# A pre-norm attention and mixture-of-experts layer on one core: the router's product, its logits and the order of some queues are changed

## The chip, the core and the metric

The kernel runs on one core of a Trainium2 chip. TensorE (PE) multiplies, VectorE (DVE), ScalarE (ACT) and GpSimd (POOL) work elementwise, SyncE (SP) issues most of the DMAs. Each engine takes its instructions strictly in the order written and waits on semaphores. The metric is the device time of one execution in microseconds (us).

## The reference, cut to what matters

`x` is 8 x 2048 tokens of 256 numbers, float32.

```python
x = x + attn(layernorm(x))            # linear attention: K^T V per sequence, then Q times it
y = layernorm(x)                      # x2 in the kernel
scores = sigmoid(y @ Wr)              # 256 -> 8 router scores
idx = top_k(scores + router_bias, 2); w = scores[idx] / (sum + 1e-9); cw = scatter(w)
hid = silu(y @ Wg[e]) * (y @ Wu[e])   # e = 0..3, inner width 128
routed = sum_e cw[e] * (hid @ Wd[e]) + (cw[4] + cw[6]) * y + cw[7] * relu(y)
out = x + routed + causal_conv4(y) + conv_b
```

## The kernel before, in words

The 16,384 tokens are 32 groups of 512 (four tiles of 128 tokens; eight sequences of four groups). One body is written out for each of the steps n = 7 to 39; the head does the steps before. In one step different stages work on different groups, as `LAG` says: L (statistics and norm 1), A (Gram matrix and transposes of the normed input), Q (query projection), B (attention product, residual, norm 2), R (transposes of x2, router, routing weights), C (the four experts), Y (the last expert's down product, output). So a group that passes B in step n passes R in n+1 and C in n+2. Every fourth step (n = 9, 13, ... 33) is a chain step, in which the matrix of a new sequence is also made out of the Gram matrix (`chain_gramT`, `chain_p1`, `chain_et`, `chain_f`). In the last steps stages go off one after the other: L after n = 31, A after 32, B after 36, R after 37, C after 38.

Products that must be exact are made in float32r out of a high part, which ACT copies, and a remainder (`_lo`), which DVE or POOL subtracts: `three` issues three passes. `gate_up(st, k)` is 2 x 3 passes of 512 columns for one expert's gate (k even) or up (k odd) product; `down(st, stage, e)` is 12 passes of 256 columns and waits for `hid_lo` of expert e. The chain of one expert is: PE gate and up products, ACT `silu`, POOL `gate_weight` (times the routing weight `cwb`), DVE `hidden`, ACT `hid_high`, then `hid_low` (DVE for experts 0 and 2, POOL for 1 and 3), PE `down`.

The routing of the next group runs beside it, in each step: PE `x2_transpose` 0 and 1 with `down(Y, 3)` between them, `gate_up` 2, `router` (eight float32 matmuls of 8 columns, the transposed x2 as weights; L509), ACT `logits_copy`, POOL `power` (e to the minus logits with ALU.pow, L1287, and plus one, L1291), DVE `route` (L1025 to L1052, top 2 and weights `cw`), PE `weights_transpose`, ACT `weights_copy`, SP a DMA to HBM (L333) and one DMA (L340) that spreads the four rows over all partitions into `cwb`, for which POOL's `gate_weight(0)` of the next step waits.

The hand-written orders that matter: on POOL `gate_weight` 0 and 1, `power`, `gate_weight` 2, `hid_low` 1, `norm1_factors`, `gate_weight` 3, the DMA that adds relu to `acc` (L1318), `norm2_factors`, `hid_low` 3, `skip_factors`. On DVE `conv_tap` 0, `norm1_stats`, `x2T_low` 0, `conv_tap` 1, `x2T_low` 1, `output`, `hidden` 0, `conv_tap` 2, `hid_low` 0, `hidden` 1, `hidden` 2, `route`, `hid_low` 2, `residual`, `norm2_stats`, `hidden` 3, `q_low`, `xnT_low`. `residual` needs the attention product alone, but stands behind `route` in DVE's queue.

Of the kernel before, what the change touches and what calls it, by code (L numbers as in the profile page):

```python
# [92 lines left out]


# [9 lines left out]
def program(nc, x, wq, wkT, wvT, woT, wr, rbias, wg, wu, wd, convwb, cw_rows, out):  # L104
# [17 lines left out]
    with ctx:  # L122
# [15 lines left out]
        wr_sb = sb("wr_sb", [P, HC, NE])  # L138
        wgu_hi = sb("wgu_hi", [P, 2, EM, HC, I], F32R)
# [41 lines left out]
        logits = sb("logits", [P, TG * NE])  # L181
# [44 lines left out]
        cwb_loaded = [sem(f"cwb_loaded{k}") for k in range(2)]  # L226
# [40 lines left out]
        halo_ready = sem("halo_ready")  # L267
        router_done = sem("router_done")
        logits_ready = sem("logits_ready")
# [42 lines left out]
        def _(sp):  # L312
# [15 lines left out]
            def spread_weights(st):  # L328
# [59 lines left out]
        def _(pe):  # L388
# [74 lines left out]
            def xn_transpose(st, c):  # L463
# [10 lines left out]
                elif g == 2:  # L474
                    if c == 0:
                        pe.wait_ge(logits_ready, 1)
# [61 lines left out]
            def attention(st, h):  # L538
# [10 lines left out]
                else:  # L549
                    pe.wait_ge(logits_ready, st.before("R", 1, 1))  # L550
# [52 lines left out]
            def head():  # L603
# [25 lines left out]
                router(r)  # L629
                xn_transpose(at("A", 2, NG), 0)  # L630
# [18 lines left out]
            def body(st):  # L649
                c_on, y_on, r_on, a_on, b_on, m_on = (st.on("C"), st.on("Y"), st.on("R"), st.on("A"), st.on("B"),  # L650
                                                      st.chain())
                if c_on and st.later("C", 1):
# [29 lines left out]
                if b_on and not m_on:  # L682
# [5 lines left out]
                if b_on:  # L688
# [22 lines left out]
        def _(act):  # L711
# [36 lines left out]
            def split_weights():  # L748
                act.wait_ge(w_loaded, 16 * N_LOADS)
                copy(wgu_hi[:, 0].rearrange("p e c i -> p (e c i)"), wg_st.rearrange("p e c i -> p (e c i)"))\  # L750
# [89 lines left out]
            def head():  # L840
# [22 lines left out]
                logits_copy(r)  # L863
                xnT_high(at("A", 2, NG), 0)
# [14 lines left out]
            def body(st):  # L879
# [19 lines left out]
                if m_on:  # L899
                    f_copy(st)  # L900
                if c_on:
                    hid_high(st, 0)
                if c_on:
                    silu(st, 2)

# [9 lines left out]
                    hid_high(st, 1)  # L915
# [7 lines left out]
                if r_on:  # L923
                    weights_copy(st)
                if st.on("Q"):
# [7 lines left out]
                if st.on("B"):  # L933
# [7 lines left out]
        def _(dve):  # L941
# [17 lines left out]
            def hid_low(st, e):  # L959

                dve.wait_ge(hidhi_ready, st.before("C", EM, e + 1))
                v.tensor_tensor(hid_lo[:, 0], hid[:, 0], hid_hi[:, 0].bitcast(F32), ALU.subtract)\
                    .then_inc(hidlo_ready[0], 1)
# [111 lines left out]
            def split_weights():  # L1075

                dve.wait_ge(w_loaded, 16 * N_LOADS)
                dve.wait_ge(whi_ready, NSPLIT)
# [286 lines left out]
```

## Time and profile before

| | |
|---|---|
| median of three runs | 924.8 us (924.77 to 928.49) |
| the profiled execution | 928.5 us, span of its instructions 926.7 us |
| granted TensorE clock, mean | 0.982 |
| PE busy | 881.6 us, 95% |
| DVE busy | 690.0 us, 74% |
| POOL busy | 608.5 us, 66% |
| ACT busy | 602.5 us, 65% |

The busy times are unions over the span. The matmuls overlap, so a busy PE says that something was in the array, not how dense it was. The clock is a share of 2.4 GHz.

### The profile page before, as it was taken

Reading aid. Unit: us, or ns where it says so; the run is one execution under the profiler, and the core shown is the slowest. Engines: PE = TensorE matmul, PEld = TensorE weight load, DVE = VectorE, ACT = ScalarE, POOL = GpSimd, SP = SyncE. Lnnn points to the kernel's source line nnn. Section 1 sums busy time; section 2 is a strip of 40 time slices with the busy share of each in tenths; the row PEclk is TensorE's granted clock in tenths of the full one; section 3 lists DMA queues with packets and bytes.
Section 4 is the critical chain, followed back from the end, with each engine's and each line's share of the span. In section 5 each row is a group of like instructions: output and inputs, shape, how many; then the busy total and the mean of one; then the engine's idle time right before and its main releaser. Section 6 shows DMA issues by size and latency. Waiting matters only on the chain.

```text
span 926.7 us, 16363 instructions
## 1 busy us (share of the span) xinstructions
PE 881.6 (95%) x5402; PEld 767.2 (83%) x5402; DVE 690.0 (74%) x1998; ACT 602.5 (65%) x1212; POOL 608.5 (66%) x686
## 2 busy tenths in 40 slices
PE   5779999999999999999999999999999999988896
PEld 4668888888888888888898888888888888777785
DVE  5766878977787888778779877877887776666563
ACT  5675676677677667766766776676677656644543
POOL 3236776667677666777766676786667767665663
PEclk9888999999999999999999999999999999999999
DMA  9111434434234443334344442434443322333232
GB/s 288 42 69 29 130 116 137 138 115 122 62 123 128 138 137 114 102 90 129 115 138 138 119 132 52 132 115 138 137 117 113 92 69 93 112 115 107 77 92 67
DMA packets 65620, 103.83 MB, mean 112 GB/s; under 512 B 4992, under 2 KB 57344, under 8 KB 61440
## 3 DMA queue, kind: packets, MB, share of 16 engines
q1 hardware_dynamic: 60928, 86.01, 27.4%
q0 software_dynamic: 4608, 16.78, 9.6%
q8 instruction: 43, 0.70, 0.3%
q14 instruction: 41, 0.34, 0.1%
HBM read 68.96 MB, written 17.04 MB: 93 GB/s over the span
## 4 chain that ended last, share of the span: by engine, by line
PE 53%; POOL 31%; DVE 5%; ACT 5%; issue 4%; DMA 1%; POOLq 0%; ACTq 0%; DVEq 0%
POOL enx L1287 17%; POOL gate L1254 8%; PE ps_gu L391 6%; PE ps_gu L393 6%; PE ps_gu L392 6%; PE ps_gram L457 6%; PE ps_y L391 5%; PE ps_y L392 4%; PE ps_y L393 4%; POOL hid_lo L1259 4%; PE ps_sh L482 3%; PE ps_gram L459 3%; PE ps_sh L499 3%; ACT gate L720 2%; PE ps_gu L532 2%
## 5 line engine op out<-in xcount | busy, mean ns | idle before, releaser
L1254 POOL TENSOR_TENSOR gate<-gate,cwb 128x512 f32<-128x512 f32 x128 | 165.3, 1292 | 113.8 <-ACT gate L720 74.8
L391 PE MATMUL ps_gu<-x2T_hi,wgu_hi 128*128 128x512 f32 x512 | 212.2, 414 | 3.3 <-DVE hid L956 3.3
L393 PE MATMUL ps_gu<-x2T_hi,wgu_lo 128*128 128x512 f32 x512 | 203.2, 397 | 0.0
L392 PE MATMUL ps_gu<-x2T_lo,wgu_hi 128*128 128x512 f32 x512 | 202.4, 395 | 0.0
L1287 POOL TENSOR_TENSOR enx<-inv_e,logits 128x32 f32<-128x32 f32 x32 | 177.1, 5535 | 10.6 <-ACT logits L713 10.4
L956 DVE TENSOR_TENSOR hid<-ps_gu,gate 128x512 f32<-128x512 f32 x128 | 86.2, 673 | 123.8 <-POOL gate L1254 101.7
L391 PE MATMUL ps_y<-wd_hi,hid_hi 128*128 128x256 f32 x512 | 157.2, 307 | 6.6 <-POOL hid_lo L1259 3.1
L393 PE MATMUL ps_y<-wd_hi,hid_lo 128*128 128x256 f32 x512 | 145.8, 285 | 0.0
L392 PE MATMUL ps_y<-wd_lo,hid_hi 128*128 128x256 f32 x512 | 145.8, 285 | 0.0
L973 DVE SCALAR_TENSOR_TENSOR conv<-x2T,conv_w,conv 128x512 f32<-128x512 f32 x192 | 144.2, 789 | 0.0
L391 PEld LDWEIGHTS ps_gu<-x2T_hi,wgu_hi 128*128 128x128 f32 x512 | 97.3, 190 | 22.7 <-DVE hid L956 6.8
L393 PEld LDWEIGHTS ps_gu<-x2T_hi,wgu_lo 128*128 128x128 f32 x512 | 97.1, 190 | 22.4
L720 ACT ACTIVATE gate<-ps_gu 128x512 f32<-128x512 f32 x128 | 76.1, 595 | 60.7 <-PE ps_gu L393 60.7
L391 PEld LDWEIGHTS ps_y<-wd_hi,hid_hi 128*128 128x128 f32 x512 | 98.5, 192 | 20.7 <-POOL hid_lo L1259 20.1
L392 PEld LDWEIGHTS ps_gu<-x2T_lo,wgu_hi 128*128 128x128 f32 x512 | 97.4, 190 | 13.6
L1259 POOL TENSOR_TENSOR hid_lo<-hid,hid_hi 128x512 fp32r<-128x512 f32 x64 | 83.4, 1303 | 35.0 <-ACT hid_hi L713 34.8
L713 ACT ACTIVATE hid_hi<-hid 128x512 fp32r<-128x512 f32 x128 | 79.9, 624 | 34.6 <-DVE hid L956 34.6
L1232 POOL TENSOR_TENSOR mv<-mv,eps_ln 128x4 f32<-128x4 f32 x64 | 12.5, 195 | 132.9 <-DVE mv L1005 113.4
L392 PEld LDWEIGHTS ps_y<-wd_lo,hid_hi 128*128 128x128 f32 x512 | 98.5, 192 | 0.1
L393 PEld LDWEIGHTS ps_y<-wd_hi,hid_lo 128*128 128x128 f32 x512 | 98.1, 192 | 0.0
L781 ACT ACTIVATE xn<-xa,shift,rstd 128x256 f32<-128x256 f32 x128 | 66.3, 590 | 23.6 <-POOL shift L1237 23.5
L457 PE MATMUL ps_gram<-xn 128*128 128x256 f32 x256 | 77.7, 386 | 0.0
(103 smaller groups left out, 1837.6 us busy)
## 6 DMA issues: line engine op xcount, KB each, us to landing
cwb<-cw_rows SPq DMA_DIRECT2D x32, 1024.0 KB, 4.7
xa<-in_x SPq DMA_DIRECT2D x32, 512.0 KB, 6.9
acc<-in_x SPq DMA_DIRECT2D x32, 512.0 KB, 6.0
acc<-x POOLq DMA_DIRECT2D x32, 512.0 KB, 4.6
out<-acc SPq DMA_DIRECT2D x64, 256.0 KB, 2.3
cwb<-in_wg SPq DMA_DIRECT2D x4, 128.0 KB, 3.8
cwb<-in_wu SPq DMA_DIRECT2D x4, 128.0 KB, 3.6
cwb<-in_wd SPq DMA_DIRECT2D x1, 512.0 KB, 4.5
```

The lines of the kernel that those rows point to most:

```text
L391: nc.tensor.matmul(dst, a_hi, b_hi, start=start, stop=False, skip_group_check=True)
L392: nc.tensor.matmul(dst, a_hi, b_lo, start=False, stop=False, skip_group_check=True)
L393: return nc.tensor.matmul(dst, a_lo, b_hi, start=False, stop=stop, skip_group_check=True)
L457: nc.tensor.matmul(ps_gram[:, 0:H], xn[:, q, t, 0:P], xn[:, q, t, :], start=start, stop=stop, skip_group_check=True)
L713: return nc.scalar.activation(dst, src, ACT.Copy, scale=scale)
L720: nc.scalar.activation(gate[:, e % 2], ps_gu[GU_BANK[2 * e]][:, :], ACT.Silu)\
L781: nc.scalar.activation(xn[:, q, t], xa[:, q, t], ACT.Identity, bias=shift1[:, f, t:t + 1], scale=rstd1[:, f, t:t + 1]).then_inc(xn_ready, 1)
L956: v.tensor_tensor(hid[:, e % 2], ps_gu[GU_BANK[2 * e + 1]][:, :], gate[:, e % 2], ALU.mult)\
L973: v.scalar_tensor_tensor(conv[:, c], x2T[:, q, c, k:k + GT], conv_w[:, c, k:k + 1], conv[:, c], ALU.mult, ALU.add).then_inc(conv_ready, 1)
L1254: g.tensor_tensor(gate[:, e % 2], gate[:, e % 2], cwb[:, q, e], ALU.mult).then_inc(gatew_ready, 1)
L1259: g.tensor_tensor(hid_lo[:, 1], hid[:, 1], hid_hi[:, 1].bitcast(F32), ALU.subtract)\
L1287: g.tensor_tensor(enx[:, :], inv_e[:, :], logits[:, :], ALU.pow).then_inc(enx_ready, 1)
```

## The change: what it does

The router's product is turned round: the router's weights, split into a high part and a remainder side by side (`wr2`, 16 of 128 columns used, the rest zero), become the stationary operand, and four float32r passes of 512 columns give the transposed logits. The first pass needs the high part of x2T's first half, the last needs the second half's remainder. ACT copies 16 x 512 of it, PE transposes it in four pieces of 16 rows behind `gate_up(3)`, ACT copies the pieces (`parts_copy`), and POOL adds the two halves of 8 at the head of `power`. `hid_low(1)` goes from POOL to DVE, and ACT's `hid_high(1)` goes ahead of the skip and relu work. The spreading DMA becomes four, one for an expert, each with its own semaphore. In the steps in which C is on and A is not, other than a chain step (`drain`, n = 34 to 38), PE makes the attention products around `gate_up(4)`, DVE does residual and statistics ahead of `hidden(2)`, POOL issues the relu DMA and the norm 2 factors ahead of `gate_weight(3)`, ACT does norm 2 right behind `weights_copy`; where B is off (n = 37), `route` stands ahead of `hidden(2)`.

```diff
+    def drain(self):
+        return self.on("C") and not self.on("A") and not self.chain()
...
-                sp.dma_start(cwb[:, k].rearrange("p e n -> p (e n)"),
-                             rows.rearrange("a e n -> (a e n)").partition_broadcast(P))\
-                    .then_inc(cwb_loaded[k], 16)
+                for e in range(EM):
+                    sp.dma_start(cwb[:, k, e], rows[0, e].partition_broadcast(P)).then_inc(cwb_loaded[k][e], 16)
...
             def router(st):
-                pe.wait_ge(x2T_ready, st.before("R", HC, HC))
+                if st.before("R") == 0:
+                    pe.wait_ge(wrlo_out, 1)
+                b, q = ps_sh[0], st.slot("R", 2)
                 pe.wait_ge(x2Tlo_ready, st.before("R", HC, 1))
-                b, q = ps_sh[0], st.slot("R", 2)
+                for c in range(HC):
+                    if c == 1:
+                        pe.wait_ge(x2Thi_ready, st.before("R", HC, HC))
+                    nc.tensor.matmul(b[:, :], wr2[:, c], x2T_hi[:, q, c], start=(c == 0), stop=False,
+                                     skip_group_check=True)
+                    if c == 1:
+                        pe.wait_ge(x2Tlo_ready, st.before("R", HC, HC))
+                    last = nc.tensor.matmul(b[:, :], wr2[:, c], x2T_lo[:, q, c], start=False, stop=(c == HC - 1),
+                                            skip_group_check=True)
+                last.then_inc(router_done, 1)
+
+            def logits_transpose(st):
+                pe.wait_ge(logitsT_ready, st.before("R", 1, 1))
                 for t in range(TG):
-                    for c in range(HC):
-                        last = nc.tensor.matmul(b[:, t * NE:(t + 1) * NE],
-                                                x2T[:, q, c, PAD + t * P:PAD + (t + 1) * P], wr_sb[:, c],
-                                                start=(c == 0), stop=(c == HC - 1))
-                last.then_inc(router_done, 1)
+                    last = nc.tensor.transpose(ps_sh[0][:, t * 2 * NE:(t + 1) * 2 * NE],
+                                               logitsT[0:2 * NE, t * P:(t + 1) * P], ident[0:2 * NE, 0:2 * NE])
+                last.then_inc(parts_done, 1)
...
                 if c_on:
                     gate_up(st, 3)
+                if r_on:
+                    logits_transpose(st)
                 if m_on:
                     chain_f(st)
+                if b_on and drain:
+                    attention(st, 0)
                 if c_on:
                     gate_up(st, 4)
+                if b_on and drain:
+                    attention(st, 1)
...
             def logits_copy(st):
                 act.wait_ge(router_done, st.before("R", 1, 1))
-
+                copy(logitsT[0:2 * NE, :], ps_sh[0][0:2 * NE, :]).then_inc(logitsT_ready, 1)
+
+            def parts_copy(st):
+                act.wait_ge(parts_done, st.before("R", 1, 1))
                 if st.later("R", 1):
-                    act.wait_ge(enx_ready, st.before("R"))
-                copy(logits[:, :], ps_sh[0][:, 0:TG * NE]).then_inc(logits_ready, 1)
+                    act.wait_ge(logits_ready, st.before("R"))
+                copy(parts[:, :, :], ps_sh[0][:, 0:TG * 2 * NE].rearrange("p (t n) -> p t n", t=TG))\
+                    .then_inc(parts_ready, 1)
...
                 if m_on:
                     f_copy(st)
+                if r_on:
+                    parts_copy(st)
                 if c_on:
                     hid_high(st, 0)
                 if c_on:
                     silu(st, 2)
+                    hid_high(st, 1)
...
                 if m_on:
                     f_low(st)
+                drain = st.drain()
+                if c_on:
+                    hid_low(st, 1)
+                if b_on and drain:
+                    residual(st, 0)
+                    residual(st, 1)
+                    norm2_stats(st)
+                if r_on and c_on and not b_on:
+                    route(st)
                 if c_on:
                     hidden(st, 2)
...
             def power(st):
+                pool.wait_ge(parts_ready, st.before("R", 1, 1))
+                if st.later("R", 1):
+                    pool.wait_ge(enx_ready, st.before("R"))
+                g.tensor_tensor(logits[:, :, :], parts[:, :, 0:NE], parts[:, :, NE:2 * NE], ALU.add)\
+                    .then_inc(logits_ready, 1)
...
                 if c_on:
                     gate_weight(st, 2)
-                    hid_low(st, 1)
                     norm1_factors(st)
+                    if st.drain():
+                        relu_add(st)
+                        if st.on("B"):
+                            norm2_factors(st)
                     gate_weight(st, 3)
```

## Rows read from the trace of the kernel before

**Rows 1.** Windows: length, busy PE, PEld, DVE, ACT, POOL; clock; DMA share, GB/s.
```profile
74.50:774.76 700.26, 696.44 (x4389) 612.40 (x4388) 552.86 (x1599) 482.00 (x978) 488.51 (x542) 1.00 0.38 116
774.76:883.53 108.77, 97.28 (x556) 80.54 (x555) 67.77 (x201) 58.38 (x116) 70.45 (x69) 0.95 0.31 90
883.53:926.70 43.17, 34.00 (x191) 28.40 (x189) 20.97 (x46) 16.89 (x33) 21.98 (x18) 0.96 0.30 86
...
505.67:531.85 26.18, 26.07 (x167) 23.18 (x166) 20.97 (x63) 18.25 (x36) 18.81 (x21) 1.00 0.41 121
```

**Rows 2.** Timeline of POOL in one step: start, length, instruction, idle before.
```profile
505.67 5.43 POOL L1287 TENSOR_TENSOR enx<-inv_e,logits 128x32 f32<-128x32 f32 x1
...
513.01 1.30 POOL L1259 TENSOR_TENSOR hid_lo<-hid,hid_hi 128x512 fp32r<-128x512 f32 x1 [0.33 <-ACT hid_hi L713]
...
515.94 1.29 POOL L1254 TENSOR_TENSOR gate<-gate,cwb 128x512 f32<-128x512 f32 x1
...
523.14 0.20 POOL L1237 TENSOR_TENSOR shift<-negm,rstd 128x4 f32<-128x4 f32 x1
```

**Rows 3.** Timeline of PE, same step.
```profile
526.00 0.60 PE L499 MATMUL ps_sh<-ident,x 128*128 128x128 f32 x4
...
528.22 0.48 PE L391 MATMUL ps_gu<-x2T_hi,wgu_hi 128*128 128x512 f32 x1
...
529.70 1.85 PE L509 MATMUL ps_sh<-wr_sb,x2T 128*128 128x8 f32 x16
531.40 0.47 PE L391 MATMUL ps_gu<-x2T_hi,wgu_hi 128*128 128x512 f32 x1
```

**Rows 4.** Timeline of DVE, same step.
```profile
512.72 0.69 DVE L956 TENSOR_TENSOR hid<-ps_gu,gate 128x512 f32<-128x512 f32 x1 [3.88 <-POOL gate L1254]
...
513.70 0.65 DVE L1027 TENSOR_TENSOR biased<-score,bias 128x32 f32<-128x32 f32 x1
...
516.28 0.98 DVE L1043 TENSOR_SCALAR wsum_eps<-wsum 128x4 f32<-128x4 f32 x1
...
530.27 0.68 DVE L1059 TENSOR_TENSOR x2T_lo<-ps_sh,x2T_hi 128x512 fp32r<-128x512 f32 x1
```

**Rows 5.** Waits of the same step: waiter, releaser, total us, times, longest.
```profile
DVE xnT_lo L1120 <- ACT xnT_hi L713: 0.9, 2, 0.6
...
PEld ps_y L391 <- POOL hid_lo L1259: 0.5, 1, 0.5
```

**Rows 6.** Timeline of ACT, same step.
```profile
524.05 2.07 ACT L792 ACTIVATE x<-acc,shift,rstd 128x256 f32<-128x256 f32 x4
```

**Rows 7.** Timeline of DVE in the head, where POOL is idle.
```profile
55.47 0.19 DVE L1027 TENSOR_TENSOR biased<-score,bias 128x32 f32<-128x32 f32 x1
...
57.55 0.17 DVE L1043 TENSOR_SCALAR wsum_eps<-wsum 128x4 f32<-128x4 f32 x1
```

**Rows 8.** Groups of instructions, shapes apart.
```profile
L1291 POOL TENSOR_TENSOR den<-enx,one_e 128x32 f32<-128x32 f32 x32 | 8.1, 254 | 2.5
```

**Rows 9.** Timeline of POOL in a chain step, DVE's conv taps running.
```profile
452.44 5.91 POOL L1287 TENSOR_TENSOR enx<-inv_e,logits 128x32 f32<-128x32 f32 x1 [0.59 <-ACT logits L713]
```

**Rows 10.** Timelines of POOL and PE in a late step.
```profile
872.03 2.26 POOL L1235 TENSOR_TENSOR rstd<-mv,half_neg 128x4 f32<-128x4 f32 x1
...
875.35 0.73 PE L499 MATMUL ps_sh<-ident,x 128*128 128x128 f32 x2 [1.64 <-ACT x L792]
```

**Rows 11.** Timelines of SP and POOL, last exchange of routing weights.
```profile
895.74 0.33 SPq L333 DMA_DIRECT2D cw_rows<-cwT  x1
899.37 0.34 SPq L340 DMA_DIRECT2D cwb<-cw_rows  x1
...
904.57 2.49 POOL L1254 TENSOR_TENSOR gate<-gate,cwb 128x512 f32<-128x512 f32 x2 [4.26 <-DMA cwb<-cw_rows]
```

**Rows 12.** Timelines of PE and DVE in the first step of the loop.
```profile
69.18 2.34 PE L509 MATMUL ps_sh<-wr_sb,x2T 128*128 128x8 f32 x16 [1.80 <-DVE x2T_lo L1059]
...
71.28 0.68 DVE L1059 TENSOR_TENSOR x2T_lo<-ps_sh,x2T_hi 128x512 fp32r<-128x512 f32 x1
```

More of the change, by code:

```diff
@@ L180, in program @@
         x2T_lo = sb("x2T_lo", [P, 2, HC, GT], F32R)
-        logits = sb("logits", [P, TG * NE])
+        logitsT = sb("logitsT", [2 * NE, GT])
+        parts = sb("parts", [P, TG, 2 * NE])
+        logits = sb("logits", [P, TG, NE])
         enx = sb("enx", [P, TG * NE])
@@ L225, in program @@
         cw_stored = sem("cw_stored")
-        cwb_loaded = [sem(f"cwb_loaded{k}") for k in range(2)]
+        cwb_loaded = [[sem(f"cwb_loaded{k}_{e}") for e in range(EM)] for k in range(2)]
         zeroed = sem("zeroed")
@@ L549, in attention @@
                 else:
-                    pe.wait_ge(logits_ready, st.before("R", 1, 1))
+                    pe.wait_ge(parts_ready, st.before("R", 1, 1))
                 if h == 0:
@@ L681, in body @@
                     down(st, "C", 0)
-                if b_on and not m_on:
+                if b_on and not m_on and not drain:
                     attention(st, 0)
@@ L687, in body @@
                     attention(st, 0)
-                if b_on:
+                if b_on and not drain:
                     attention(st, 1)
@@ L749, in split_weights @@
                 act.wait_ge(w_loaded, 16 * N_LOADS)
+                act.wait_ge(wr_zeroed, 1)
+                copy(wr2[:, :, 0:NE], wr_sb[:, :, :]).then_inc(wrhi_out, 1)
                 copy(wgu_hi[:, 0].rearrange("p e c i -> p (e c i)"), wg_st.rearrange("p e c i -> p (e c i)"))\
@@ L863, in head @@
                 logits_copy(r)
+                parts_copy(r)
                 xnT_high(at("A", 2, NG), 0)
@@ L924, in body @@
                     weights_copy(st)
+                if st.on("B") and st.drain():
+                    norm2(st)
                 if st.on("Q"):
@@ L932, in body @@
                     xnT_high(st, 1)
-                if st.on("B"):
+                if st.on("B") and not st.drain():
                     norm2(st)
@@ L961, in hid_low @@
                 dve.wait_ge(hidhi_ready, st.before("C", EM, e + 1))
-                v.tensor_tensor(hid_lo[:, 0], hid[:, 0], hid_hi[:, 0].bitcast(F32), ALU.subtract)\
-                    .then_inc(hidlo_ready[0], 1)
+                k = e % 2
+                v.tensor_tensor(hid_lo[:, k], hid[:, k], hid_hi[:, k].bitcast(F32), ALU.subtract)\
+                    .then_inc(hidlo_ready[k], 1)
             def conv_tap(st, n):
@@ L1187, in body @@
                     f_low(st)
+                drain = st.drain()
+                if c_on:
[6 more added lines that the diff above has]
+                    route(st)
                 if c_on:
                     hidden(st, 2)
-                if r_on and c_on:
+                if r_on and c_on and b_on:
                     route(st)
@@ L1193, in body @@
                     hid_low(st, 2)
-                if b_on:
+                if b_on and not drain:
                     residual(st, 0)
@@ L1309, in body @@
                     gate_weight(st, 2)
-                    hid_low(st, 1)
                     norm1_factors(st)
+                    if st.drain():
+                        relu_add(st)
+                        if st.on("B"):
+                            norm2_factors(st)
                     gate_weight(st, 3)
-                if c_on:
-                    pool.wait_ge(ident_added, st.before("C", TG, TG))
-                    pool.wait_ge(relu_ready, st.before("C", TG, TG))
-                    k, q = st.slot("C", 4), st.slot("C", 2)
-                    g.dma_start(acc[:, k].rearrange("p t n -> p (t n)"), x2[:, q].rearrange("p t n -> p (t n)"),
-                                accum_op=ALU.add).then_inc(relu_added[q], 16)
-                if st.on("B"):
+                if c_on and not st.drain():
+                    relu_add(st)
+                if st.on("B") and not st.drain():
                     norm2_factors(st)
                 if c_on:
-                    hid_low(st, 3)
+                    last_low(st)
                 if r_on:
```

29 lines of the change are left out of this document (22 added, 7 removed).

## The prediction, made before the change was run

> **What bounds the kernel now.** I read the windows first. The long middle, steps 8 to 33, is 700.3 of 926.7 us, 26.93 a step with the chains in it; a step without chain work is 26.18 us, and PE is busy in 26.07 of it at full clock [rows 1]. The reader is to see there that the middle is on PE, and that the late steps are not: the four behind n = 33 take 108.8 us, 27.2 each, though PE has no Gram matrix, query product or transposes of xn left in them and is busy only 97.3, at clock 0.95 [rows 1]. Those run at the latency of a loop.
>
> Then I followed the loop in the timelines of one middle step, from the start of POOL's pow at 505.67 to the next at 531.85. Two loops come back to pow. Loop A: pow, gate 2, `hidden(2)` at 512.72, route, residual, statistics, norm factors ready at 523.34 [rows 2, 4], norm 2 on ACT from 524.05 [rows 6], x2 transposes at 526.00, down and `gate_up(2)`, router at 529.70 [rows 3], pow. Between 523.34 and 524.05 it has 0.7 us of slack. Loop B stays on DVE: from `hidden(2)` it works until `x2T_low(1)` ends at 530.95 [rows 4], 18.23 us with 0.9 us of waits for ACT [rows 5]; before the change nothing in the router needs that end. So three bounds lie within a microsecond: PE, A and B. The price of any edit is what it does to the largest.
>
> **The change, part by part.**
>
> *PE's work.* Out: the router, from 529.70 to the next product at 531.40, 1.70 us. In: four passes of 512 columns. `gate_up(2)` is six of them from 528.22 to 529.70, at most 0.247 each [rows 3], so 0.95. In too: four transposes; as the router's 16 rows take 0.106 each [rows 3], 0.43 (0 at the best, 0.9 at half clock). Net -0.3 us. PE also stops waiting for POOL's `hid_low(1)`, which its queue shows as up to 0.5 [rows 5]; I take 0.3. PE alone would need 25.6.
>
> *The way from router to pow.* Before, from router's start to pow 529.70 to 531.85, 2.15 us [rows 1, 3]. After: 0.95, `gate_up(3)` that stands ahead of the transposes 1.4 (ACT's first copy hides under it, as a copy is under 0.7 us; norm 2 does four of 256 columns in 2.07 [rows 6]), transposes 0.43, second copy and handing over 0.3, POOL's addition 0.32 with its hand-over, priced by L1291's 0.25 [rows 8]. That is 3.4, so +1.25 for loop A. The addition may lie under DVE's `conv_tap(2)`; a four-column rstd takes 2.26 in a late step beside such taps [rows 10], so at the worst the addition costs 2 more. In a chain step pow itself starts under those taps and takes 5.91 for 5.43 [rows 2, 9]. After the change it does so in each step: +0.45 in A and B.
>
> *POOL loses `hid_low(1)`, 1.30 us.* By itself it is not what holds up the loops; what follows is. `route`'s small operations are held while a POOL operation runs. L1027 takes 0.65 and ends at 514.35, as `hid_lo` does at 514.31; L1043 takes 0.98 and ends at 517.26, `gate_weight(3)` at 517.23 [rows 2, 4]. In the head, with POOL idle, they take 0.19 and 0.17 [rows 7]. After the change `hid_low(1)` is gone, and `gate_weight(3)` comes about 1.3 us sooner, under max and match_replace. So -1.27 in A and B, at the most; 0 if the gate still falls on a small operation. The trace gives both cases; I take the full value, since a gate 1.3 us sooner ends ahead of L1043.
>
> The Trainium skill (SBUF — State Buffer, section "Who interferes with whom") says that a DVE instruction with two SBUF inputs contends with a GpSimd one that reads SBUF, and that the one that comes second blocks for the other's whole length. The rows on L1043 and L1027 agree. Taken to the letter the page speaks against moving the subtraction: on DVE it reads two SBUF tiles while POOL is inside a 5.4 us pow. That is the first rival's stronger form. By the rule the sum would have `hidden(2)` held as well.
>
> *DVE gains 0.69 us* (the length of its other subtractions [rows 4]) in a gap of 3.88 us that it has before `hidden(2)` [rows 4]. Cost 0 while the gap is there. `hid_high(1)` moved ahead feeds it, and delays nothing that ends last, ACT having 18.25 busy of 26.18 [rows 1].
>
> *The fourth pass waits for `x2T_low(1)`,* a new wait. Behind it on PE stand `gate_up(3)` and the transposes, and ACT and POOL wait for those. This closes loop B: pow to `hidden(2)` 7.05 + 0.45; DVE 18.23 - 0.9 (waits that depend on PE, free when PE is ahead) - 1.27 = 16.06; then last pass with semaphore 0.3, `gate_up(3)` 1.4, transposes 0.43, copy 0.3, addition 0.32. Sum 26.3. Loop A: 26.18 - 0.7 + 1.25 + 0.45 - 1.27 = 25.9. PE 25.6. Loop B is the new bound, 26.3 against 26.18.
>
> *Middle:* 26 steps x 0.12 = +3.1. Chain steps: `parts_copy` stands behind `f_copy` and PE's `chain_f`; about 1.2 us in the loop, but PE's own excess is in the 26.93 already, and PE now has slack to give back. I take +0.1 for each of seven, +0.7.
>
> *First step of the loop:* PE began its next product at 71.37; the last pass cannot start before `x2T_low(1)` ends at 71.96 [rows 12]. +1.0.
>
> *Four spreading DMAs.* SP issues one in 0.34 [rows 11], so three more, 1.0 us, ahead of `load_acc` and `load_x`, which are wanted a step or more later: 0. In the middle `gate_weight(0)` feeds `hidden(0)`, which stands behind `output`, so an earlier first row gives 0 too.
>
> *Late steps, n = 34 to 36.* Residual, statistics and norm 2 no longer wait for route on DVE. But ACT's norm 2 stands behind `weights_copy`, and that waits for PE's transpose of `cw`, which waits for route. From pow: gate 2 done at 7.4, route done at 11.9 (the gate may now hold L1043), `cw` transposed and copied by 12.4. PE's list up to there is four products 5.6, two downs 2.9 and attention 1.0 at half of 0.247 for a pass of 256, conv's transposes 0.9, from 0.7 ahead of pow: done at 9.7, idle about 2.5. In the present trace, after 1.64 us of idleness there [rows 10], PE runs at half clock (mean 0.95 in this window [rows 1]). I charge half clock for the 4 us behind the gap, +2.1. From 12.6: down 1.45, two products 2.8, x2 transposes 0.9, down(Y) 1.45, `gate_up(2)` 1.4, and the 2.1, is 22.7; then the last pass and what stands behind it, 2.75: 25.4 against 27.2. Three such intervals x -1.8 = -5.4; without the half clock 23.3, -12. The interval behind chain step 33 keeps the old order: A decides it, +0.3.
>
> *The end.* For the last exchange the small DMA goes out at 895.74 and the spreading one at 899.37, 3.6 us later, behind the relu DMA; the gate begins at 904.57, 5.2 us later [rows 11]. After: the relu DMA goes out ahead of gate 3, out of the way, so the gap between the two should be near half, -1.8; and the gate waits for a quarter of the data, about half of 5.2, -2.6. Of these 4.4 PE's own list, which has to be worked off in between, hides some; I take four fifths, -3.6 (0 to -6, since `hid_low(1)` no longer stands behind ACT's relu there either).
>
> *Sum:* +3.1 + 0.7 + 1.0 + 0.3 - 5.4 - 3.6 = -3.9. On the profiled execution's 928.5 that is 924.6 (its span, 926.7, lies 1.8 inside). The median of the runs is 3.7 below that execution, so I forecast 924.8 - 3.9 = 920.9, rounded 921.
>
> **The rivals.**
>
> *Slower, 937:* loop B is longer than reckoned. What decides is whether route is really freed of POOL. If `gate_weight(3)` still falls on one of its operations, 0.8 of the 1.27 is lost, and B is 27.05, +0.8 x 26 = +21 less the late steps' 9: 937. It decides from B = 26.4 on. For it: the three bounds are so close that nothing absorbs it. Against: a shift of 1.3 us is more than L1043's distance. If, as the page's rule would have it, pow blocked DVE's two-input operations, `hid_low(1)` would run only behind pow and `hidden(2)` 0.7 later, the same size, 0.7 x 26 = +18 less 9: 934. Against that speaks that `hidden(2)` waits 3.88 us for nothing but the gate [rows 4].
>
> *Faster, 903:* B is not binding. If pow and addition do not meet the taps, B is 25.8, and PE's 25.6 to 25.8 sets the step: -0.45 x 26 = -12, with late steps and end -9: 903.
>
> *No change, 925:* the late steps give nothing (half clock and `cw` eat it) and the middle stays: -4 + 4. For it: norm 2 is still behind route, through `weights_copy`. Against: 27.2 has room above any of the bounds.
>
> **How the numbers follow.** Forecast 0.42, own range 912 to 929; slower 0.23; faster 0.20; no change 0.15. A measurement tells about 0.5% from no change, that is 920.2 to 929.4. The forecast lies near that edge: of its 0.42, 0.21 is faster, 0.20 the same, 0.01 slower. With the others (no change: 0.01 faster, 0.13 same, 0.01 slower): faster 0.42, same 0.33, slower 0.25. Range 901 to 938: it takes in both outer rivals' values and leaves about 0.1 above and as much below.
>
> **What would show it.** Right: in the middle PE waits some tenths for the second `x2T_lo` ahead of the router's last pass; the `wsum_eps` operation near 0.2; pow near 5.9; pow starts 26.2 to 26.4 apart; late steps near 25.4 with a PE gap of 2.5 us before the `cw` transpose; two small DMAs under 2.5 us apart at the end. Wrong: pow starts 26.8 or more apart (slow rival), or a PE with no gaps and 25.7 (fast rival); late steps at 23 or 27.

## The result and the profile after

The changed kernel takes 961.2 us (median of four runs, 959.0 to 962.4) against 926.2 for the one before (four runs), a ratio of 1.037 [1.034, 1.041]. The forecast was 921 with a range up to 938. The profiled execution took 959.0 us, its span is 957.2.

The windows of the changed kernel, cut at the starts of POOL's pow as in [rows 1] (middle, late steps, end, one ordinary step):

```profile
75.31:811.12 735.81, 703.24 (x4193) 595.14 (x4192) 570.38 (x1626) 503.95 (x1008) 472.18 (x542) 1.00 0.38 110
811.12:915.75 104.63, 92.20 (x521) 77.70 (x520) 71.89 (x207) 60.08 (x119) 64.83 (x69) 0.95 0.34 96
915.75:957.20 41.45, 31.87 (x182) 27.34 (x180) 23.77 (x45) 16.31 (x32) 20.32 (x16) 0.91 0.29 77
528.21:556.19 27.98, 26.45 (x159) 22.43 (x158) 21.95 (x64) 19.05 (x37) 18.35 (x21) 1.00 0.41 123
```

Between the same pow starts the kernel before had 702.93, 108.77 and 43.17 us, and its first pow of the loop came at 71.83 (the first window of [rows 1] begins at 74.50, 2.7 us behind that pow, so that its 26.93 a step is 27.04 from pow to pow). So the 30.5 us of span are +3.5 ahead of the first pow, +32.9 in the 26 middle intervals, -4.1 in the four late ones and -1.7 at the end. The loss is all in the middle: an ordinary step went from 26.18 to 27.98, and PE, which was busy in 26.07 of 26.18 [rows 1], now has 1.5 us of gaps. Four steps with one chain step among them, on which the experiments below are compared, took 107.4 us before (27.96, 27.04, 26.19, 26.18) and 113.2 after (29.79, 27.49, 27.98, 27.97). The step behind a chain step, which starts its pow clear of DVE's taps, lost 0.45, each of the other three 1.8.

One such step in the timelines. POOL, to set beside [rows 2]:

```profile
527.52 0.62 POOL L1351 TENSOR_TENSOR logits<-parts 128x32 f32<-128x32 f32 x1 [1.69 <-ACT parts L743]
528.21 5.77 POOL L1354 TENSOR_TENSOR enx<-inv_e,logits 128x32 f32<-128x32 f32 x1
...
534.27 1.29 POOL L1308 TENSOR_TENSOR gate<-gate,cwb 128x512 f32<-128x512 f32 x1
...
537.20 1.30 POOL L1308 TENSOR_TENSOR gate<-gate,cwb 128x512 f32<-128x512 f32 x1
...
555.51 0.60 POOL L1351 TENSOR_TENSOR logits<-parts 128x32 f32<-128x32 f32 x1 [1.71 <-ACT parts L743]
```

DVE, to set beside [rows 4]:

```profile
529.99 0.69 DVE L1004 TENSOR_TENSOR hid_lo<-hid,hid_hi 128x512 fp32r<-128x512 f32 x1 [0.70 <-ACT hid_hi L743]
535.60 0.69 DVE L997 TENSOR_TENSOR hid<-ps_gu,gate 128x512 f32<-128x512 f32 x1 [4.91 <-POOL gate L1308]
...
536.58 0.19 DVE L1069 TENSOR_TENSOR biased<-score,bias 128x32 f32<-128x32 f32 x1
...
537.27 1.26 DVE L1075 COPY two<-top 128x8 f32<-128x8 f32 x1
...
539.76 0.17 DVE L1085 TENSOR_SCALAR wsum_eps<-wsum 128x4 f32<-128x4 f32 x1
...
546.44 0.82 DVE L1154 COPY x2T<-x2T 128x6 f32<-128x6 f32 x1
...
552.21 0.67 DVE L1101 TENSOR_TENSOR x2T_lo<-ps_sh,x2T_hi 128x512 fp32r<-128x512 f32 x1
...
554.60 1.39 DVE L1015 SCALAR_TENSOR_TENSOR conv<-x2T,conv_w,conv 128x512 f32<-128x512 f32 x2
555.98 0.69 DVE L1004 TENSOR_TENSOR hid_lo<-hid,hid_hi 128x512 fp32r<-128x512 f32 x1
```

PE, to set beside [rows 3]:

```profile
552.93 0.50 PE L525 MATMUL ps_sh<-x2T_lo,wr 128*128 128x512 f32 x1 [0.51 <-DVE x2T_lo L1101]
...
554.75 0.41 PE L532 MATMUL ps_sh<-ident,logitsT 16*128 16x16 f32 x4
```

The reader is to see three things. The two operations that the prediction freed from POOL are free (0.19 and 0.17, as in [rows 7]), but `gate_weight(3)`, at 537.20 to 538.50, now lies on the copy into `two` between them, which takes 1.26 and ends at 538.53. The last pass of the router waits 0.51 us for `x2T_low(1)`. And the addition takes 0.60 us, beside the conv taps that run until 555.99; POOL cannot begin pow until it is done, and pow takes 5.77 instead of 5.43.

### The profile page after: what moved, and what is told of

It is laid out like the page before. It is cut to its first block, busy times and chain, and to the rows that moved or that the text cites. A ratio compares the mean times of both kernels' runs of the same rounds, so it can differ in the third digit from the quotient of the medians.

```text
span 957.2 us, 16111 instructions
## 1 busy us (share of the span) xinstructions
PE 878.9 (92%) x5146; PEld 741.6 (77%) x5146; DVE 713.8 (75%) x2031; ACT 626.7 (65%) x1245; POOL 583.3 (61%) x687
## 4 chain that ended last, share of the span: by engine, by line
POOL 30%; DVE 29%; PE 25%; issue 8%; ACT 7%; DMA 1%; POOLq 0%; ACTq 0%; DVEq 0%
POOL enx L1354 18%; ACT x L824 4%; POOL gate L1308 4%; DVE stats L1044 4%; DVE acc L1036 4%; PE ps_gu L401 4%; DVE two L1075 4%; PE ps_gu L403 4%; PE ps_gu L402 4%; POOL rstd L1290 3%; DVE hid L997 2%; PE ps_sh L509 2%; PE ps_y L401 2%; DVE marked L1078 2%; PE ps_y L403 2%
## 5 line engine op out<-in xcount | busy, mean ns | idle before, releaser
L1354 POOL TENSOR_TENSOR enx<-inv_e,logits 128x32 f32<-128x32 f32 x32 | 181.9, 5684 | 2.5
L401 PE MATMUL ps_y<-wd_hi,hid_hi 128*128 128x256 f32 x512 | 154.2, 301 | 3.9 <-DVE hid_lo L1004 3.0
L1015 DVE SCALAR_TENSOR_TENSOR conv<-x2T,conv_w,conv 128x512 f32<-128x512 f32 x192 | 142.2, 778 | 0.0
L1004 DVE TENSOR_TENSOR hid_lo<-hid,hid_hi 128x512 fp32r<-128x512 f32 x96 | 69.1, 720 | 39.9 <-ACT hid_hi L743 39.9
```

Source lines behind the costliest of these rows:

```text
L401: nc.tensor.matmul(dst, a_hi, b_hi, start=start, stop=False, skip_group_check=True)
L1004: v.tensor_tensor(hid_lo[:, k], hid[:, k], hid_hi[:, k].bitcast(F32), ALU.subtract)\
L1015: v.scalar_tensor_tensor(conv[:, c], x2T[:, q, c, k:k + GT], conv_w[:, c, k:k + 1], conv[:, c], ALU.mult, ALU.add).then_inc(conv_ready, 1)
L1354: g.tensor_tensor(enx[:, :], inv_e[:, :], logits[:, :, :].rearrange("p t e -> p (t e)"), ALU.pow)\
```

## The experiments

Ratios are to the kernel before, run on the same chip. All but the second are the changed kernel with the edit shown; `...` marks lines left out. A period is four steps as above.

**The router of before.**

```diff
-                    nc.tensor.matmul(b[:, :], wr2[:, c], x2T_hi[:, q, c], start=(c == 0), stop=False,
-                                     skip_group_check=True)
...
+                        last = nc.tensor.matmul(b[:, t * NE:(t + 1) * NE],
+                                                x2T[:, q, c, PAD + t * P:PAD + (t + 1) * P], wr_sb[:, c],
+                                                start=(c == 0), stop=(c == HC - 1))
...
-                g.tensor_tensor(logits[:, :, :], parts[:, :, 0:NE], parts[:, :, NE:2 * NE], ALU.add)\
-                    .then_inc(logits_ready, 1)
```

The transposes of the logits and `parts_copy` go with them.

> The changed kernel with the router of before (eight float32 matmuls, one copy, no transposes of logits, no addition on POOL); all else as changed (late order, VectorE's remainder of expert 1, early hid_high, four spreading DMAs, route order). Theory 1, the loop router - logits - pow - hidden(2) - route - ... - second x2T_lo - router, which only the new router closes, costs the time: a middle step falls from 27.98 to 26.0 us (PE's bound), the late steps keep their gain, and the kernel is at 908 to 918 us, faster than before. Theory 2, the moved work (the remainder on VectorE, early hid_high) costs it: a middle step stays above 27 us and the time above 940 us.

903.3 us, ratio 0.976 [0.971, 0.981]. Windows of this kernel: middle, late steps, one ordinary step.

```profile
71.81:762.00 690.19, 690.19 (x4395) 615.87 (x4395) 560.19 (x1630) 481.22 (x979) 458.09 (x516) 1.00 0.41 118
762.00:860.40 98.40, 91.44 (x556) 78.91 (x555) 70.68 (x206) 58.15 (x116) 61.83 (x65) 0.98 0.34 98
...
602.75:628.56 25.81, 25.81 (x166) 23.26 (x166) 21.32 (x65) 18.22 (x36) 17.54 (x22) 1.00 0.43 126
```

PE is busy in all of the middle. Everything in the change but the router is a gain of 2.4%; the router alone costs 2.17 us an ordinary step (27.98 against 25.81), and the first pow is back at 71.81.

**The router alone,** put into the kernel before: `hid_low(1)` on POOL, `hid_high(1)` late, one spreading DMA, no `drain`.

```diff
...
-                    hid_low(st, 1)
...
                     gate_weight(st, 2)
+                    low_pool(st, 1)
```

The line taken out is DVE's, the one put in POOL's.

> The kernel before with the new router alone (four float32r passes, copy, four transposes, copy, POOL's addition); order, remainders and DMA as before. Theory 1: a middle step of 28 us or a little more, since hid_lo(1) of POOL now holds VectorE's small operations too; 965 to 975 us, as the late steps gain nothing. Theory 2: about as before, 925 to 935 us.

999.9 us (991.7 to 1008.1), ratio 1.076 [1.070, 1.082], periods of 116 to 119. The waits of two steps (500 to 560 us):

```profile
PE ps_y L402 <- POOL hid_lo L1311: 4.0, 2, 2.0
```

Pow now ends later against PE's list, POOL's `hid_low(1)` stands behind pow and gate 2, and PE's down waits 2.0 us a step for it. The middle is 761.4 us against the changed kernel's 735.8, 1.0 a step; with the router of before, moving `hid_low(1)` and `hid_high(1)` gives 0.37 (below). So the move is worth more with the new router, as far as the single spreading DMA, in which this run differs too, has no share in it; that was not run by itself.

**The copy into `two` as a reduction,** which reads one input.

```diff
-                done(v.tensor_copy(two8[:, :, 0:2], top8[:, :, 0:2]))
+                done(v.tensor_reduce(two8[:, :, 0:2], top8[:, :, 0:2].unsqueeze(3), AXX, ALU.max))
```

> The changed kernel; route's copy of the two best scores is made by a tensor_reduce (max over one element) in its place, the same values. Theory 1 with the collision as its larger part: gate_weight(3) no longer holds it, the next operation that it can hold starts close to the gate's end, so route and with it a middle step are 0.8 to 1.1 us shorter, 26.9 to 27.2 us; 932 to 942 us. Rival: the 1.26 us of that copy is hidden by slack elsewhere (norm 2 or PE): under 0.3 us a step, over 952 us.

937.6 us, ratio 1.012 [1.010, 1.014]; step 27.12, 0.86 less. DVE and POOL of this kernel:

```profile
523.15 0.16 DVE L1075 TENSOR_REDUCE two<-top 128x8 f32<-128x8 f32 x1
```

```profile
523.09 1.30 POOL L1308 TENSOR_TENSOR gate<-gate,cwb 128x512 f32<-128x512 f32 x1
```

The gate begins 0.06 us ahead of the operation, in the changed kernel 0.07, and the reduction takes 0.16 where the copy took 1.26. That the gate held it, and that this is 0.86 of the step, is shown. The addition (0.60) and pow (5.79) are as in the changed kernel.

**`x2T_low(1)` ahead of `conv_tap(1)` on DVE.**

```diff
+                if r_on:
+                    x2T_low(st, 1)
                 if c_on:
                     conv_tap(st, 1)
-                if r_on:
-                    x2T_low(st, 1)
```

> The changed kernel; VectorE makes the second x2T remainder ahead of conv_tap(1) in place of behind it. Theory 1 (the fourth pass waits on VectorE, so its end is on the loop): the wait of 0.5 us and the restart vanish, a middle step is 0.5 to 0.7 us shorter, then the loop by norm 2 binds; 943 to 948 us. Rival (the loop by norm 2 binds already and the wait is filled slack): under 0.2 us a step, 956 to 961 us.

960.0 us, ratio 1.036 [1.034, 1.039]. PE no longer waits ahead of the last pass, but the taps now lie under `gate_weight(1)` (two take 2.45 instead of 1.39), `hidden(0)` comes late, and in three steps of four PE waits 1.9 us for it. The fourth step, without this wait, takes 26.6 us, the others 27.6 to 30.4; the middle is 741.8 against 735.8. So this run does not show what the wait for `x2T_low(1)` is worth: it puts another in its place.

**The transposes ahead of `gate_up(3)`.**

```diff
+                if r_on:
+                    logits_transpose(st)
                 if c_on:
                     gate_up(st, 3)
-                if r_on:
-                    logits_transpose(st)
```

> The changed kernel with the four logits transposes ahead of gate_up(3) in place of behind it: PE waits for ScalarE's copy (about 0.7 us), but 1.4 us of product leave the way from router to pow. If that way is on the loop in each step, a middle step is 0.7 us shorter, 27.3 us, and the kernel takes 940 to 946 us. Rival: PE's new wait of 0.7 us costs as much as it gives, under 0.3 us a step, 953 to 961 us.

964.6 us, ratio 1.037 [1.033, 1.042]; step 28.25. POOL and DVE of this kernel:

```profile
561.87 1.84 POOL L1351 TENSOR_TENSOR logits<-parts 128x32 f32<-128x32 f32 x1 [1.07 <-ACT parts L743]
563.79 5.44 POOL L1354 TENSOR_TENSOR enx<-inv_e,logits 128x32 f32<-128x32 f32 x1
```

```profile
561.60 1.39 DVE L1015 SCALAR_TENSOR_TENSOR conv<-x2T,conv_w,conv 128x512 f32<-128x512 f32 x2
562.92 0.67 DVE L1004 TENSOR_TENSOR hid_lo<-hid,hid_hi 128x512 fp32r<-128x512 f32 x1
```

The parts are there earlier, and the addition that comes just behind the taps' start is held until the subtraction behind them is done too: 1.84 us. Arriving sooner gave nothing in the middle (749.6 us against 735.8); in the four late intervals, 99.0 against 104.6, it did.

**The sum of the halves on PE:** the transposes by the identity become products with a 16 x 8 matrix that adds row e and row 8 + e; no addition on POOL.

```diff
-                    last = nc.tensor.transpose(ps_sh[0][:, t * 2 * NE:(t + 1) * 2 * NE],
-                                               logitsT[0:2 * NE, t * P:(t + 1) * P], ident[0:2 * NE, 0:2 * NE])
+                    last = nc.tensor.matmul(ps_sh[0][:, t * NE:(t + 1) * NE],
+                                            logitsT[0:2 * NE, t * P:(t + 1) * P], fold[:, :], start=True, stop=True)
...
-                g.tensor_tensor(logits[:, :, :], parts[:, :, 0:NE], parts[:, :, NE:2 * NE], ALU.add)\
-                    .then_inc(logits_ready, 1)
```

> The changed kernel; the four transposes are matmuls of 8 columns by a folding matrix (two identities on top of each other), so they give the sum, and POOL's addition is gone. The addition takes 0.6 us beside VectorE's taps in the trace and 0.08 of handing over: a middle step 0.6 to 0.7 us shorter, 27.3 us; with twice the PE rows (0.4 us more) on the way back, net 0.2 to 0.3; 947 to 956 us. Rival: pow then starts beside the taps and loses what was won: 958 us or more.

950.6 us, ratio 1.022 [1.018, 1.026]; step 27.54, 0.44 less; pow 5.43 in each step.

**The last pass reads the first half's remainder again,** so that it does not wait for `x2T_low(1)`. The logits lack the second half's remainder.

```diff
-                    if c == 1:
-                        pe.wait_ge(x2Tlo_ready, st.before("R", HC, HC))
-                    last = nc.tensor.matmul(b[:, :], wr2[:, c], x2T_lo[:, q, c], start=False, stop=(c == HC - 1),
+                    last = nc.tensor.matmul(b[:, :], wr2[:, c], x2T_lo[:, q, 0], start=False, stop=(c == HC - 1),
```

> The changed kernel; the router's last pass reads the first half's remainder once more in place of the second's (so the router leaves out one of four terms and has a wrong one), and does not wait for VectorE's second x2T remainder; nothing else moves. Loop B, by way of VectorE's list, is then open. If it alone binds, a middle step falls by the pass's wait and restart and on until the loop by norm 2 binds: 0.5 to 0.7 us shorter, 940 to 948 us. Rival, the loop by norm 2 binds as hard: under 0.2 us a step, 955 to 961 us.

966.6 us, ratio 1.039 [1.035, 1.043]; step 28.22. POOL of this kernel; DVE's taps run from 555.12:

```profile
555.23 2.00 POOL L1349 TENSOR_TENSOR logits<-parts 128x32 f32<-128x32 f32 x1 [0.89 <-ACT parts L741]
557.31 5.44 POOL L1352 TENSOR_TENSOR enx<-inv_e,logits 128x32 f32<-128x32 f32 x1
```

The same as with the transposes first. The wait that the prediction took for the new bound can be taken away, and the time does not fall: what the addition is held for takes its place (2.00 for 0.60, the step 28.22 for 27.98).

**Three together:** reduction, sum on PE, and these products ahead of `gate_up(3)`.

> The changed kernel with all three: the copy in route as a reduce, the transposes ahead of gate_up(3), the sum on PE. If the terms add (1.0, 0.7, 0.3 of 27.98), a middle step is 26.0 to 26.2 us, at PE's bound, and the kernel 908 to 918 us. Rival: another loop binds after the first two; 925 us or more.

965.2 us, ratio 1.038 [1.032, 1.043], although two of the three edits gain when made alone. Ordinary steps of 25.9, 27.4 and 28.9 us alternate. Windows of 2 us in one of the long ones:

```profile
614.00:616.00 2.00, 2.00 (x10) 1.42 (x8) 2.00 (x4) 1.58 (x3) 0.00 (x0) 1.00 0.91 286
616.00:618.00 2.00, 0.98 (x5) 0.50 (x4) 2.00 (x4) 0.70 (x2) 1.27 (x1) 1.00 0.85 302
618.00:620.00 2.00, 2.00 (x10) 1.76 (x10) 2.00 (x4) 0.72 (x2) 0.94 (x1) 0.69 0.80 281
620.00:622.00 2.00, 2.00 (x6) 1.54 (x5) 0.60 (x2) 0.00 (x0) 2.00 (x1) 0.50 0.00 1
```

With nothing between the last pass and the small products, PE idles 0.34 ahead of the pass and 0.68 ahead of the products, and behind this the granted clock falls to 0.50, the lower level of 1.2 GHz. That is the step of 28.9. In the one of 27.4 the gaps are 0.19 and 0.68, the clock stays at 1.00, and the step is still 0.7 above that of the next run, in which only the place of the products differs. So the clock is a part of the loss and not all of it; pow takes 5.82 there for 5.43, and the rest is open.

**Reduction and sum on PE,** the products behind `gate_up(3)`.

> The changed kernel with two edits that each gained by themselves: the copy into two as a reduction (-0.86 a step) and the sum of the two logits halves made on PE by a 16 x 8 matrix (-0.44 a step); the transposes stay behind gate_up(3), unlike in the run of three edits. Theory 1 (the last pass of the router, route and the way to pow are one loop, and the gains lie one behind the other in it): they add, 27.98 - 0.86 - 0.44 = 26.7 for an ordinary step, 28.5 for a chain step, about 928 us, ratio 1.00. Theory 2 (the run of three lost its gain not to the moved transposes but to the two edits meeting each other): the step stays at 27.4 with longer ones between, above 950.

930.7 us, ratio 1.004 [1.002, 1.006]; step 26.69 (1.29 less, 0.86 + 0.44 = 1.30), period 109.0. Windows: an ordinary and a chain step.

```profile
486.68:513.37 26.69, 26.44 (x163) 23.03 (x162) 20.72 (x63) 18.73 (x38) 17.48 (x20) 1.00 0.42 119
540.07:569.15 29.08, 29.08 (x180) 25.09 (x179) 21.17 (x63) 20.22 (x45) 17.46 (x20) 1.00 0.39 110
```

The two losses add. PE is busy in all of the chain step; in the ordinary one a single gap is left, 0.25 us ahead of the last pass, for `x2T_low(1)`. The loop from pow to pow is 7.05 to `hidden(2)`, 16.41 on DVE to the end of `x2T_low(1)` and 3.23 from there: it still closes in the ordinary step.

**Router of before, no `drain`.**

```diff
-        return self.on("C") and not self.on("A") and not self.chain()
+        return False
```

> The changed kernel with the router of before, and without the other order in the steps n = 34 to 38 (no drain, no early route). Theory 1 (the late gain of the change is made by that order): the middle stays at 690.2, the four intervals behind n = 33 go from 98.4 back to 106 to 108, total 911 to 914. Theory 2 (the late gain comes from hid_low(1) leaving POOL): the intervals stay near 99, total 903 to 905.

911.4 us, ratio 0.983 [0.979, 0.987]. Windows: the late steps and the end.

```profile
761.89:870.36 108.47, 96.11 (x556) 80.52 (x555) 70.60 (x206) 58.43 (x116) 65.15 (x65) 0.95 0.32 89
870.36:909.60 39.24, 32.40 (x190) 27.15 (x189) 22.46 (x48) 16.98 (x33) 19.50 (x17) 1.00 0.35 94
```

The late order is worth 108.47 - 98.40 = 10.1 us, and the end without it is 3.9 shorter than before (43.17), from the four DMAs, the two moves of expert 1 and a granted clock of 1.00 for 0.96; they can't be told apart here. A part of the 10.1 is clock too (0.98 against 0.95).

**Router of before, `hid_low(1)` and `hid_high(1)` back in their places.**

> The changed kernel with the router of before, and hid_low(1) back on POOL behind gate 2, hid_high(1) back behind relu. Theory 1 (the middle gains 0.36 a step because PE no longer waits for that remainder and route is less held): the step goes back to 26.18, middle 702, total 913 to 916. Theory 2 (the four spreading DMAs give the middle's gain): step 25.82, total 903 to 905.

913.8 us, ratio 0.984 [0.980, 0.987]; step 26.19, middle 699.8 against 690.2. The two moves together are 26.19 - 25.82 = 0.37 a step.

**`conv_tap(2)` behind `hid_low(0)` and `hidden(1)`.**

```diff
-                    conv_tap(st, 2)
                     hid_low(st, 0)
                     hidden(st, 1)
+                    conv_tap(st, 2)
```

> The changed kernel with conv_tap(2) moved behind hid_low(0) and hidden(1) on DVE, so that it no longer runs beside POOL's addition and the start of pow. Theory 1 (collisions of DVE's two-input operations with POOL's addition and pow cost about 0.35 each): addition 0.25 instead of 0.60, pow 5.44 instead of 5.78, ordinary step 27.3, total 942 to 946. Theory 2 (the addition meets hid_low(0) instead, which now waits for ACT's hid_high(0) right behind parts_copy, and hidden(1) comes later): step 27.9 or more, total 958 to 966.

984.8 us, ratio 1.061 [1.055, 1.067], period 116.3. The addition takes 0.25 and pow 5.44 in each step, as theory 1 had it, but neither theory had what PE's timeline shows, the products that carry the conv into `ps_y`:

```profile
546.68 1.09 PE L451 MATMUL ps_y<-ident,conv 128*128 128x128 f32 x8 [1.88 <-DVE conv L1015]
```

The tap has a reader on PE, which now gets there 1.9 us too early, and the holds that were saved are lost in this wait.

**No wait, no copy and no addition:** reduction, sum on PE, and the last pass with the first half's remainder.

> The changed kernel with the reduction into two and the sum of the halves on PE, and in it the last router pass reading the first half's remainder again, so that it no longer waits for x2T_low(1) (the logits then lack the second half's remainder). Theory 1 (the wait for x2T_low(1) was worth something all along, and its removal gave nothing before only because POOL's addition then was held for 2.0 us; here there is no addition): the gap of 0.25 us ahead of the last pass goes, and the step is PE's own list, 26.3 to 26.4 against 26.69, total 918 to 922. Theory 2 (the wait is hidden, loop A carries the step): 26.6 to 26.7, 928 to 931.

925.2 us, ratio 0.998 [0.996, 1.000]; period 109.2 (27.04, 29.93, 25.94, 26.28), the same as with the wait. Two of its pows, on POOL, and what DVE does at the second one's start:

```profile
594.01 5.78 POOL L1349 TENSOR_TENSOR enx<-inv_e,logits 128x32 f32<-128x32 f32 x1 [1.54 <-ACT logits L742]
...
620.28 6.55 POOL L1349 TENSOR_TENSOR enx<-inv_e,logits 128x32 f32<-128x32 f32 x1 [1.54 <-ACT logits L742]
```

```profile
619.54 1.39 DVE L1014 SCALAR_TENSOR_TENSOR conv<-x2T,conv_w,conv 128x512 f32<-128x512 f32 x2
620.87 0.67 DVE L1003 TENSOR_TENSOR hid_lo<-hid,hid_hi 128x512 fp32r<-128x512 f32 x1
```

The 0.25 us of wait are gone (26.28 where theory 1 said 26.3 to 26.4), but pow then starts under the taps and is held in turn: 6.55 is 1.12 over 5.43, and the next step is 27.04. The total that theory 1 gave, 918 to 922, was missed.

**Router of before and the reduction.**

> The changed kernel with the router of before, and the copy into two as a reduction. Theory 1 (with that router PE is the bound, 25.81 of 25.82 busy, and the gate holds another operation of route anyway): nothing in the ordinary step, some tenths in chain and late steps, 900 to 904, the same as without the reduction. Theory 2 (route is still in the loop): -0.3 a step, 893 to 896.

904.0 us, ratio 0.974 [0.970, 0.979], the same as without the reduction. DVE and POOL of this kernel:

```profile
613.77 0.16 DVE L1052 TENSOR_REDUCE two<-top 128x8 f32<-128x8 f32 x1
614.72 1.12 DVE L1057 SCALAR_TENSOR_TENSOR raw<-marked,score 128x32 f32<-128x32 f32 x1
```

```profile
614.49 1.29 POOL L1285 TENSOR_TENSOR gate<-gate,cwb 128x512 f32<-128x512 f32 x1 [0.73 <-ACT gate L735]
```

With this router the gate comes 0.8 us later, behind `two` (a copy there takes 0.17 anyway), and holds `raw`, 1.12 for 0.19, whether `two` is a copy or a reduction. So nothing was freed, and the run says nothing on what a freed DVE is worth. But a hold of the same size is in the fastest two versions: with PE busy in all of the step it does not bind.


## Why the prediction was wrong

*The step that failed is "I take the full value, since a gate 1.3 us sooner ends ahead of L1043".* It does end ahead of L1043, and L1027 and L1043 did give back their 1.27. But the gate, 1.3 us long, still lies beside `route`, and the rows of `route` between those two, which the prediction put down as max and match_replace, hold a copy that is held just as well. It took 1.26 for 0.17 (its length with the router of before), so the 1.27 shrank to 0.18. The shift was off too: counted from `hidden(2)` the gate began at 3.22 us before [rows 2, 4] and at 1.60 after, 1.6 sooner and not 1.3, as POOL's wait of 0.33 for ACT ahead of `hid_low(1)` [rows 2] went with that operation. An estimate from these rows: 1.3 sooner would be 1.92, just behind the copy (1.67 to 1.84), and the gate would have held `raw` (from 2.61) instead, for some 0.4. By this estimate the full 1.26 hangs on 0.07 us. And L1043, which the prediction saw held, reads one tile and not two: its own row said that an operation need not have two inputs to be held. The Trainium skill (SBUF — State Buffer, section "Who interferes with whom") names copies among the operations that can take the shared port pair and says that `tensor_reduce` on trn2 never does; 1.26 against 0.16 under the same gate agrees. The slow rival had this mechanism, at 0.8 us a step; it measures 0.86. Its own total, 937, is 24 short of the result, since it was only the first of two losses in the middle. The stronger form of that rival, pow blocking DVE, did not come: `hid_low(1)` at 529.99 lies inside pow and takes 0.69.

*The addition.* "0.32, priced by L1291's 0.25", with the held case named and left out of the sum. It takes 0.60, 0.68 with the hand-over, and without it the step is 0.44 shorter. Pow itself came near the forecast, 5.77 for 5.88, though it starts as the taps end and beside `hid_low(0)`. The last stretch, from the end of `x2T_low(1)` (552.88) to pow (556.19), is 3.31 for 2.75.

*Loop B* was the right loop, and its first term right: pow to `hidden(2)` 7.39 (7.50). DVE from there to the end of `x2T_low(1)` took 17.28 for 16.06: 1.09 is `two`, 0.54 the halo copy (L1154, 0.82 beside POOL's `hid_lo` of 545.94; 0.28 in the step before the change, where 0.25 of that subtraction was left as it began), less some 0.4 of conv taps and smaller differences (the second pair of taps takes 1.39 here and took 1.65 in the step before the change). 7.39 + 17.28 + 3.31 = 27.98. With copy and addition mended it is 26.69, so that 1.3 of the 1.67 us between 26.31 and 27.98 are these two. But that the wait for `x2T_low(1)` closes the loop is not the whole of it: without that wait the middle was no shorter, in neither of two runs (740.6 against 735.8 us, 709.6 against 709.3). What fixes pow's start is also where the small POOL operations fall against DVE's taps, and coming sooner moves them further in: the addition took 0.60, 1.84 and 2.00 as it came 0.91, 0.27 and 0.11 us behind the start of the two taps. There is a pattern in these rows that no run tested by itself. Where DVE's subtraction begins as the taps end (555.98 and 555.99), POOL gets in between the two: 0.60, and 5.78 for pow. Where it begins 0.06 or 0.07 ahead of their end (620.87 and 620.93, 562.92 and 562.99), POOL stays out until the subtraction is done: 1.84, 2.00, 6.55.

*PE's work.* -0.3 was right in size: the router's products took 1.71 from start to start, the four passes and transposes some 1.5 (0.23 a pass and 0.45 for the transposes, with the restart behind them). The forecast that PE would come out at 25.6 could not show itself behind loop B. PE at 25.81 with the router of before is shown; so is the 0.3 a step that the prediction gave to PE's wait for POOL's `hid_low(1)` (0.37, with `hid_high(1)` moved as well).

*Chain steps* were forecast at +0.1 and came out at +1.8, the ordinary step's own loss.

*First step:* +1.0 was forecast, +3.5 measured. From the end of `x2T_low(1)` to pow it is 4.60 us for 2.75, in which PE, behind a wait of 1.97 us ahead of the last pass, ran at a granted clock of 0.50 throughout. The prediction charged half clock behind a gap in the late steps, and did not here.

*Late steps:* -5.4 and +0.3 forecast, -4.1 measured (intervals 27.40, 26.16, 26.31, 24.76 for 26.45, 27.53, 27.41, 27.38). The first interval lost 0.95 where 0.3 was forecast, the other three gained 5.1 of the 5.4. That the order makes the gain is shown by the run without `drain`, with the router of before. That the sum came so near is in part luck: 25.4 was forecast for each, with half clock behind the gap, and the last of 24.76 ran at a granted clock of 1.00. The gap ahead of the `cw` transpose was forecast at 2.5 and is 2.79. With the router of before the order is worth 10.1 us, the clock's share with it. With the new router it was not run by itself; the new router alone takes 110.7 in these four intervals, the changed kernel 104.6.

*End:* -3.6 was forecast. With the router of before and no `drain` it is -3.9; in the changed kernel the clock is 0.91 there ([rows 1] had 0.96) and -1.7 is left. The DMA part came as forecast: the first spreading DMA goes out 1.39 us behind the small one (3.63 before), and `gate_weight(0)`, which waited 4.26 for the DMA [rows 11], now waits for ACT. That the clock takes back the rest is not shown.

In the sum: the middle, forecast at +3.8, measured +32.9, is 29.1 of the error; the first step 2.5, the end 1.9, the late steps 1.0.

*What stays open.* With both holds out the new router's period is 109.0, the old one's 105.9. A part of the 3.1 is the eight small products that replace the four transposes (1.05 us for 0.41, about 0.6 a step), so it belongs to the mended version and not to the change. For the changed kernel itself, how much is left to the longer way alone can't be separated: with each hold taken out, something else moved.

## What to carry to other kernels

When an edit moves a long POOL operation by a microsecond, do not ask whether it leaves the operation that it held, but list, one by one, what DVE issues in the place where it will lie, with the kind and the inputs of each; a copy of 8 columns can cost as much as the POOL operation is long. A small POOL operation on the critical way between two engines should be priced at what DVE runs beside it, and where DVE's list is full, arriving sooner may only mean being held for longer: turn the operation into one that does not contend (a reduction, a product on PE) rather than speed up what feeds it. And time a change of several parts by part: here the parts without the router gained 2.4% together, and the router hid it.

## What the hardware showed that was not expected

Pow, 5.43 us on POOL, reads two SBUF inputs, yet DVE's operations inside it, the two-input subtraction of 529.99 among them, ran at their usual 0.69 us. Pow was longer only where a DVE operation with two SBUF inputs was running as it began: 5.43 or 5.44 without one, 5.78 with the last 0.5 us of the taps or of the subtraction ahead of it, 6.55 with the end of the taps and a subtraction. The Trainium skill (SBUF — State Buffer, section "Who interferes with whom") has the second one blocked for the whole instruction; by that DVE would have stood still for most of pow. The measurement decides: pow held nothing of DVE's, while a gate of 1.30 us held a copy for all of its length. What sets the two apart no run here shows. In the other direction DVE kept a POOL operation out across three of its own instructions, two taps and a subtraction: the 128x32 addition took 2.00 us for 0.25.
